# Normalising the attention output first in VectorE's step, in front of the masked maxima

## The chip, the cores and the metric

The kernel runs on one core of a Trainium2 chip. The metric is the device time of one execution in microseconds (us), lower is better. Engines are named as in the profile: PE is TensorE (matmuls), PEld its weight loads, DVE is VectorE, ACT is ScalarE, POOL is GpSimd, SP is SyncE, which here only issues DMAs.

## The reference: a feed-forward pass, windowed attention, a feed-forward pass

Tokens are 8 x 512 rows of width 512. The reference adds three things to them one after the other, each taken from a layer-normalised copy:

```
x = x + 0.5 * ffn(layernorm(x))        # pass A
x = x + attn(layernorm(x))             # attention, pass B
x = x + 0.5 * ffn(layernorm(x))        # pass C

ffn:  gate, up = split(x @ ternary(w_gate_up).T);  h = silu(gate) * up
      return rms_norm(h) @ ternary(w_proj).T                      # hidden width 2048
attn: 32 heads of width 16; a query sees its own and the previous 128 keys
      probs = softmax(where(valid, q @ k.T * scale, min));  return (probs @ v) @ Wo.T
```

## The kernel before

**Blocks and steps.** The rows are cut into 32 blocks of 128 tokens; 4 blocks make a sequence. A prologue of about 150 us turns and quantises the weights. After it the five engines each run their own list of steps, 4 to about 282; eight steps belong to a block, and in one step TensorE does work of several blocks at different stages. The order inside a step is written by hand for each engine (the functions `step_of`), and engines meet only at semaphores. Nothing reorders it.

**TensorE's step.** First half of up for a quarter of a feed-forward pass (`ps_g`), down for the quarter of two steps ago, second half of up (`ps_u`), then scores of a group of 4 heads for the next step, then the product of probabilities and V (`prob_v`) of the group of three steps ago, and in some steps a projection (Q, K, V or output). In the names below `ps_gu` is the pair of banks with `ps_g` and `ps_u`, `ps_yy` holds down's results, `ps_s` scores, and `ps_om` the pair of `ps_o` (product with V) and `ps_m` (projections). Passes A and C have their quarters in alternating steps, so that each step has one; before the first blocks have reached C and after the last has left A, only one of the two passes is there.

**VectorE's step.** The masked maxima of the scores (L876, four pairs: the masked scores to `masked`, the maximum to `row_max`); the low half of Q, K or V in some steps (L854); the low half of the probabilities of the group before (`prob`, L850); in every second step, from step 16 on, the normalisation of the attention output of 8 heads; the gated `hid` (L859: reads `ps_g`, writes `hid`); sometimes the added attention output (L978); the second `hid` (L865: reads `ps_u`); sometimes the low half of the attention output (`oh`), the added feed-forward output (L898) and a layer norm's statistics; last the low half of the hidden values (`hh`).

**The normalisation** is `normalise_o`: it waits for the second product with V of its pair of groups (`p_pv`), sums the two halves of the product (`o_sum`, L886), takes the reciprocal of the row sums (`row_inv`, L887), and multiplies both into `o_norm` (L891). Four of them make a block's attention output. TensorE waits for it (`d_on`) before the next pair of groups overwrites `ps_o`, and after the fourth ScalarE copies `o_norm` to `oh`.

**What waits for what around it.** Scores of the next group overwrite `ps_s`, so TensorE waits for the step's maxima (`d_mx`). ScalarE turns the maxima into `exp_bias`, takes four exponentials in place, later makes `prob` of them. The first half of up in the next step overwrites `ps_g`, so it waits for this step's gated `hid` (`d_gate`). SP transposes each half of the probabilities, the normalised tokens (`xt_A`, `xt_B`, `xt_C`), `hh` and `oh` by DMA, one list for all. GpSimd normalises the tokens (`xhat`, L539) and takes their low half (`xh`, L544).

Of the kernel before, what the change touches and what calls it, by code (L numbers as in the profile page):

```python
# [24 lines left out]
def macaron(nc, x, Wq, Wk, Wv, Wo, w_gate_up, w_proj, out):  # L25
# [47 lines left out]
    NORM = PV + 1  # L73
# [7 lines left out]
    with ExitStack() as ctx:  # L81
# [180 lines left out]
        def need(eng, s, n):  # L262
            if n > 0:
                eng.wait_ge(s, n)

        def block_at(step, offset):

            b, rest = divmod(step - offset, 8)
            return b if rest == 0 and 0 <= b < NB else None

        def group_at(step, offset):

            n = step - offset
            return (n // 8, n % 8) if 0 <= n < 8 * NB else (None, None)
# [49 lines left out]
        def complete(s, step, behind):  # L324

            t, b, c = ffn_at(step - behind)
            return b if t == s and c == NC - 1 else None
# [53 lines left out]
        def head_view(ap):  # L381
            return ap.rearrange("p (h d) -> p h d", d=DK)
# [5 lines left out]
        def prob_part(ap, b):  # L388

            return ap[:, first_half(b):2, :, :]  # L390
# [358 lines left out]
        def _(dve):  # L749
# [132 lines left out]
            def normalise_o(b, ct):  # L882
                dve.wait_ge(p_pv, 8 * b + 2 * ct + 2)
                o = ps_o[:, 0:8 * VW].rearrange("p (h t) -> p h t", h=8)
                parts = o[:, :, 0:2 * DK].rearrange("p h (t d) -> p h d t", t=2)
                dve.tensor_reduce(o_sum[:, :, :], parts, AX.X, ALU.add).then_inc(d_osum, 1)  # L886
                dve.reciprocal(row_inv[:, :].unsqueeze(2), o[:, :, 2 * DK:VW]).then_inc(d_rinv, 1)  # L887
                dve.wait_ge(d_osum, 4 * b + ct + 1)
                dve.wait_ge(d_rinv, 4 * b + ct + 1)
                need(dve, d_ol, b)  # L890
                dve.tensor_tensor(out=head_view(o_norm[:, ct * P:(ct + 1) * P]), in0=o_sum[:, :, :],  # L891
                                  in1=row_inv[:, :].unsqueeze(2).to_broadcast([P, 8, DK]),
                                  op=ALU.mult).then_inc(d_on, 1)
# [50 lines left out]
            attention_scales()  # L944

            def step_of(step):
                b, g = group_at(step, SCORES)
                if b is not None:
                    masked_max(b, g)

                b = block_at(step, Q_AT + 1)
# [3 lines left out]
                b = block_at(step, K_AT + 1)  # L955
# [3 lines left out]
                b = block_at(step, V_AT + 1)  # L959
# [3 lines left out]
                b, g = group_at(step, PROB)  # L963
                if b is not None:
                    need(dve, t_pl[g % 2], 16 * (4 * b + g // 2))
                    take_lo(prob_part(prob[:, g % 2, 1, :, :, :], b), prob_f32(b, g),
                            prob_part(prob[:, g % 2, 0, :, :, :], b), a_ph, 8 * b + g + 1, d_pl)

                b, g = group_at(step, NORM)
                if b is not None and g % 2:  # L970
                    normalise_o(b, g // 2)

                def output_lo(b):
                    take_lo(oh[:, 1, :], o_norm[:, :], oh[:, 0, :], a_oh, b + 1, d_ol)
# [19 lines left out]
                b = block_at(step, WO_AT + 1)  # L994
# [17 lines left out]
                b = block_at(step, SPLIT_O)  # L1012
                if b is not None and b < LAST:
                    output_lo(b)
                b = complete("A", step, 2)
                if b is not None:
                    add_ffn("A", b, d_x1)
                b = complete("C", step, 2)
                if b is not None:
                    add_ffn("C", b, d_x3)  # L1020
                b = block_at(step, LN_B)
                if b is not None and b > 0:
                    norm_stats("B", b, d_x1, b + 1)
                b = block_at(step, LN_C)
                if b is not None and b < LAST:
                    norm_stats("C", b, d_x2, b + 1)
                b = block_at(step, LN_A)
# [9 lines left out]
            for step in range(FIRST_STEP, STEPS):  # L1037
                step_of(step)
# [239 lines left out]
```

## Time and profile before

| | |
|---|---|
| median of 3 runs | 2048.57 us (2048.05 to 2049.78) |
| profiled execution, its time | 2045.48 us |
| its span | 2043.7 us, so 1.8 us lie around it |
| TensorE, VectorE, ScalarE, GpSimd busy | 94%, 78%, 73%, 26% of the span |
| TensorE's mean granted clock | 0.984 of full |

In a row of the timeline the first number is the start in us from the start of the span, the second the duration, then engine, line of the kernel, operation, output and inputs, and the count. What stands in square brackets is the time for which the engine was idle just before, and what ended it; no bracket means that it wasn't. In the list of waits a row is: waiting engine and operation, what it waited for, then the total in us, how many times, the longest. Matmul ends are modelled, and a row's duration can reach 0.1 us over the start of the next on the same engine.

### The profile page before, as it was taken

To read this page: it belongs to the slowest core of one execution; us is meant where nothing else is said; L and a number is where in the kernel's file an instruction comes from. 1 tells how busy PE (TensorE), PEld (TensorE's weight loads), DVE (VectorE), ACT (ScalarE), POOL (GpSimd) and SP (SyncE) were. 2 spreads that over 40 slices of the span, in tenths; PEclk is the share of its full clock that TensorE was granted. 3 is DMA by queue.
4 is the path that set the end of the run, shared out by engine and by line. 5 is a ranking of instruction groups with operands and counts; after the bars stand their busy time and mean duration, and the time that the engine had idled before them with its cause. 6 is when DMAs were issued, how large, how long until landed. Compare 5 with 4: busy or idle time off the path is not lost. (4 is left out here: it accounts for less than half of the span.)

```text
span 2043.7 us, 37471 instructions
## 1 busy us (share of the span) xinstructions
PE 1918.7 (94%) x12447; PEld 897.5 (44%) x12688; DVE 1596.0 (78%) x4079; ACT 1485.7 (73%) x2871; POOL 527.8 (26%) x559
## 2 busy tenths in 40 slices
PE   6588899999999999999999999999999999999887
PEld 4353344444444444444444444444444444444332
DVE  7967788778887888788887888778887788777763
ACT  7837777777777777777776777777776777768762
POOL 2012232222232322322223223222223232221110
PEclk9889999999999999999999999999999999999888
DMA  6336898779887987677886788869886788768762
GB/s 232 125 67 120 150 154 142 126 140 159 149 150 129 153 144 148 134 145 147 154 157 124 137 149 152 148 129 154 157 150 123 139 150 163 141 122 153 135 127 55
DMA packets 1031648, 287.81 MB, mean 141 GB/s; under 512 B 1016096, under 2 KB 1017120, under 8 KB 1030944
## 3 DMA queue, kind: packets, MB, share of 16 engines
q1 hardware_dynamic: 1031456, 285.41, 75.5%
q8 instruction: 101, 1.65, 0.3%
q14 instruction: 91, 0.75, 0.1%
HBM read 25.17 MB, written 8.39 MB: 16 GB/s over the span
## 5 line engine op out<-in xcount | busy, mean ns | idle before, releaser
L731 ACT ACTIVATE masked<-masked,exp_bias,exp_scale 128x256 f32<-128x256 f32 (+1 forms) x1024 | 503.9, 563 | 8.6
L1094 PE MATMUL ps_yy<-wp_t,ht 128*128 128x512 bf16 x1978 | 480.7, 383 | 13.6 <-DMA ht<-hh 11.5
L1048 PE MATMUL ps_gu<-wgu_t,xt_A 128*128 128x512 bf16 x1940 | 473.2, 381 | 10.3 <-DVE hid L859 2.9
L1048 PE MATMUL ps_gu<-wgu_t,xt_C 128*128 128x512 bf16 x1958 | 475.6, 381 | 7.0 <-DVE hid L859 1.1
L605 ACT ACTIVATE hh<-hid 128x512 f16<-128x512 f32 x256 | 160.7, 628 | 271.7 <-DVE hid L865 266.1
L850 DVE TENSOR_TENSOR prob<-masked,prob 128x1024 f16<-128x1024 f32 (+1 forms) x256 | 342.4, 1338 | 9.5 <-ACT prob L743 9.5
L876 DVE CUSTOM_DVE_ANT_0 masked<-ps_s,mask 128x256 f32<-128x256 f32 (+1 forms) x1024 | 337.2, 385 | 0.6 <-PE ps_s L1084 0.6
L865 DVE SCALAR_TENSOR_TENSOR hid<-ps_gu,h_scale_u,hid 128x512 f32<-128x512 f32 x252 | 189.1, 750 | 159.9 <-PE ps_gu L1048 142.5
L1094 PEld LDWEIGHTS ps_yy<-wp_t,ht 128*128 128x128 f16 x2016 | 197.5, 98 | 252.6 <-DMA ht<-hh 13.2
L1048 PEld LDWEIGHTS ps_gu<-wgu_t,xt_A 128*128 128x128 f16 x2048 | 198.2, 98 | 241.8 <-issue 5.3
L1048 PEld LDWEIGHTS ps_gu<-wgu_t,xt_C 128*128 128x128 f16 x2048 | 194.1, 98 | 228.4 <-issue 6.9
L544 POOL TENSOR_TENSOR xh<-xhat,xh 128x512 f16<-128x512 f32 x94 | 132.7, 1412 | 595.1 <-ACT xh L605 595.1
L850 DVE TENSOR_TENSOR hh<-hid,hh 128x512 f16<-128x512 f32 x256 | 176.1, 688 | 129.3 <-ACT hh L605 126.6
L743 ACT ACTIVATE prob<-masked 128x1024 f16<-128x1024 f32 (+1 forms) x256 | 239.3, 935 | 0.5
L609 ACT ACTIVATE hid<-ps_gu 128x512 f32<-128x512 f32 x256 | 150.1, 586 | 86.6 <-PE ps_gu L1048 82.9
L859 DVE SCALAR_TENSOR_TENSOR hid<-hid,ps_gu 128x512 f32<-128x512 f32 x256 | 174.1, 680 | 11.3 <-ACT hid L609 10.9
L1106 PE MATMUL ps_om<-v,pt 128*128 128x33 f16 x3584 | 131.9, 178 | 27.9 <-DVE o_norm L891 26.0
L666 ACT ACTIVATE squares<-hid 128x512 bf16<-128x512 f32 x256 | 157.1, 614 | 0.0
L1106 PEld LDWEIGHTS ps_om<-v,pt 128*128 128x128 f16 x3584 | 107.3, 96 | 77.4 <-issue 71.6
L726 ACT ACTIVATE exp_bias<-row_max,prob_bias,neg_exp_scale 128x4 f32<-128x4 f32 x256 | 97.5, 381 | 11.2 <-DVE row_max L876 8.0
L1084 PE MATMUL ps_s<-kt,qt 48*128 48x256 f16 (+1 forms) x1024 | 93.8, 262 | 10.3 <-DVE row_max L876 10.3
L535 POOL TENSOR_TENSOR rstd_B<-var_eps_B,neg_half 128x1 f32<-128x1 f32 x32 | 28.5, 890 | 282.0 <-DVE var_eps_B L845 282.0
(148 smaller groups left out, 1875.6 us busy)
## 6 DMA issues: line engine op xcount, KB each, us to landing
stream<-in_L_attn_x_dram SPq DMA_DIRECT2D x32, 256.0 KB, 3.4
pt<-prob SPq DMA_TRANSPOSE x512, 3.3
out_dram<-stream SPq DMA_DIRECT2D x32, 256.0 KB, 2.4
prob<-in_L_ffn_w_gate_up_dram SPq DMA_DIRECT2D x4, 1024.0 KB, 5.6
ht<-hh SPq DMA_TRANSPOSE x256, 3.2
stream<-in_L_ffn_w_gate_up_dram SPq DMA_DIRECT2D x3, 1024.0 KB, 5.4
stream<-in_L_ffn_w_proj_dram SPq DMA_DIRECT2D x2, 1024.0 KB, 4.9
prob<-in_L_ffn_w_proj_dram SPq DMA_DIRECT2D x2, 1024.0 KB, 5.4
```

The lines of the kernel that those rows point to most:

```text
L605: act.activation(dst, src, ACT.Copy, scale=scale).then_inc(done, 1)
L609: act.activation(hid[:, n % 2, :], ps_g[:, :], ACT.Tanh, scale=0.5 * 2.0 ** -XS_LOG2).then_inc(a_tanh[s], 1)
L666: act.activation(squares[:, n % 2, :], hid[:, n % 2, :], ACT.Square, accum_out=sq_quarter[s][:, c:c + 1]).then_inc(a_sq[s], 1)
L731: t = act.activation(p, p, ACT.Exp, bias=exp_bias[:, 4 * g + h:4 * g + h + 1], scale=exp_scale[:, 0:1])
L743: act.activation(prob_part(prob[:, g % 2, 0, :, :, :], b), prob_f32(b, g), ACT.Copy).then_inc(a_ph, 1)
L850: dve.tensor_tensor(out=dst, in0=src, in1=hi, op=ALU.subtract).then_inc(done, 1)
L859: dve.scalar_tensor_tensor(out=hid[:, n % 2, :], in0=hid[:, n % 2, :], scalar=1.0, in1=ps_g[:, :], op0=ALU.add, op1=ALU.mult).then_inc(d_g ...
L865: dve.scalar_tensor_tensor(out=dst, in0=ps_u[:, :], scalar=scale, in1=hid[:, n % 2, :], op0=ALU.mult, op1=ALU.mult).then_inc(d_h[s], 1)
L876: m = dve.tensor_tensor_reduce(masked[:, g % 2, 2 * pair + o, first:2 * P], ps_s[:, o * CH + pair * 2 * P + first:o * CH + (pair + 1) * 2 ...
L1048: t = pe.matmul(bank[:, :], xt[s][:, part, k, :], wgu_t[:, k, at:at + CH], start=(k == 0 and part == 0), stop=(k == KD - 1 and part == 1))
L1094: t = pe.matmul(ps_y[s][:, :], ht[:, n % HRING, i, :], wp_t[:, 4 * c + i % 4, :], start=(c == 0 and i == 0), stop=(c == NC - 1 and i == 2 ...
L1106: t = pe.matmul(ps_o[:, at:at + VW], pt[:, g % 2, part, half, 2 * pair + o, :], v[:, at_block - 1 + half, hd, 0:VW], start=(n == 0), stop= ...
```

## The change

In VectorE's step the call of `normalise_o` moves from behind the low half of the probabilities to the head of the step, in front of `masked_max`. Its condition, its waits and its instructions are the same; no other engine's list changes.

```
             def step_of(step):
+                b, g = group_at(step, NORM)
+                if b is not None and g % 2:
+                    normalise_o(b, g // 2)
+
                 b, g = group_at(step, SCORES)
                 if b is not None:
                     masked_max(b, g)
...
                     take_lo(prob_part(prob[:, g % 2, 1, :, :, :], b), prob_f32(b, g),
                             prob_part(prob[:, g % 2, 0, :, :, :], b), a_ph, 8 * b + g + 1, d_pl)
-
-                b, g = group_at(step, NORM)
-                if b is not None and g % 2:
-                    normalise_o(b, g // 2)
```

On VectorE, in a step with the fourth normalisation of a block (`hh` closes the step before, `masked` and `row_max` are the maxima, `ps_om` the product with V); first the whole difference:

```order
 L850 TENSOR_TENSOR hh<-hid,hh 128x512
-L876 ISA masked,row_max<-ps_s,mask 128x256
...
-L850 TENSOR_TENSOR prob<-masked,prob 128x1024
-L886 TENSOR_REDUCE o_sum<-ps_om 128x128
-L887 RECIPROCAL row_inv<-ps_om 128x8
-L891 TENSOR_TENSOR o_norm<-o_sum,row_inv 128x128
+L886 TENSOR_REDUCE o_sum<-ps_om 128x128
+L887 RECIPROCAL row_inv<-ps_om 128x8
+L891 TENSOR_TENSOR o_norm<-o_sum,row_inv 128x128
+L876 ISA masked,row_max<-ps_s,mask 128x256
...
+L850 TENSOR_TENSOR prob<-masked,prob 128x1024
 L859 SCALAR_TENSOR_TENSOR hid<-hid,ps_gu 128x512
```

The three instructions of the normalisation have passed the maxima and the low half of the probabilities; the gated `hid` (L859) stands where it stood, behind all of them.

On VectorE, in a step with the low half of K (`k4`), the same three instructions are also moved past that:

```order
 L850 TENSOR_TENSOR hh<-hid,hh 128x512
+L886 TENSOR_REDUCE o_sum<-ps_om 128x128
+L887 RECIPROCAL row_inv<-ps_om 128x8
+L891 TENSOR_TENSOR o_norm<-o_sum,row_inv 128x128
 L876 ISA masked,row_max<-ps_s,mask 128x256
...
 L854 SCALAR_TENSOR_TENSOR k4<-ps_om,k4 128x32x16
 L850 TENSOR_TENSOR prob<-masked,prob 128x1024
-L886 TENSOR_REDUCE o_sum<-ps_om 128x128
-L887 RECIPROCAL row_inv<-ps_om 128x8
-L891 TENSOR_TENSOR o_norm<-o_sum,row_inv 128x128
 L859 SCALAR_TENSOR_TENSOR hid<-hid,ps_gu 128x512
```

They stand now in front of an instruction that waits for ScalarE's copy of K, where they stood behind it.

## Rows read from the trace of the kernel before

**Rows 1.** The page: span, TensorE's busy time, its granted clock in 40 slices.

```profile
span 2043.7 us, 37471 instructions
...
PE 1918.7 (94%) x12447; PEld 897.5 (44%) x12688; DVE 1596.0 (78%) x4079; ACT 1485.7 (73%) x2871; POOL 527.8 (26%) x559
...
PEclk9889999999999999999999999999999999999888
```

**Rows 2.** Waits of PE, 152 to 240, 240 to 1880, 1880 to 1980 us.

```profile
PE ps_om L1106 <- DVE o_norm L891: 7.7, 5, 1.9
PE ps_s L1084 <- DVE row_max L876: 3.8, 4, 2.4
PE ps_gu L1048 <- DMA xt_A<-xh: 1.3, 2, 0.9
...
PE ps_om L1106 <- DVE o_norm L891: 10.7, 21, 0.7
PE ps_gu L1048 <- DVE hid L859: 1.1, 7, 0.2
...
PE ps_om L1106 <- DVE o_norm L891: 7.6, 6, 2.0
PE ps_s L1084 <- DVE row_max L876: 6.5, 4, 2.2
```

**Rows 3.** Line L891: duration in ns, least, median and most; first and last start.

```profile
L891 DVE TENSOR_TENSOR o_norm<-o_sum,row_inv x128: 291/293/623, 171.9 to 1990.4; 128x128 f32<-128x128 f32 x128
```

**Rows 4.** Timeline, a step with a block's fourth normalisation, all engines.

```profile
1015.97 0.75 DVE L865 SCALAR_TENSOR_TENSOR hid<-ps_gu,h_scale_u,hid 128x512 f32<-128x512 f32 x1 [0.70 <-PE ps_gu L1048]
...
1019.03 0.42 DVE L876 CUSTOM_DVE_ANT_0 masked<-ps_s,mask 128x256 f32<-128x256 f32 x1
...
1019.69 2.08 POOL L539 TENSOR_SCALAR xhat<-stream,mean_var_B,rstd_B 128x512 f32<-128x512 f32 x1 [0.18 <-POOL rstd_B L535]
...
1020.40 0.08 DVE L876 DVE_READ_ACCUMULATOR2_ANT row_max<- 128x1 f32 x1
1020.40 1.22 DVE L850 TENSOR_TENSOR prob<-masked,prob 128x1024 f16<-128x1024 f32 x1
...
1021.54 0.42 DVE L886 TENSOR_REDUCE o_sum<-ps_om 128x128 f32<-128x256 f32 x1
...
1021.77 0.39 PE L1084 MATMUL ps_s<-kt,qt 48*128 48x256 f16 x4
...
1022.16 0.29 DVE L891 TENSOR_TENSOR o_norm<-o_sum,row_inv 128x128 f32<-128x128 f32 x1
1022.37 0.68 DVE L859 SCALAR_TENSOR_TENSOR hid<-hid,ps_gu 128x512 f32<-128x512 f32 x1
...
1022.60 0.55 PE L1106 MATMUL ps_om<-v,pt 128*128 128x33 f16 x16 [0.44 <-DVE o_norm L891]
...
1023.11 1.90 PE L1048 MATMUL ps_gu<-wgu_t,xt_C 128*128 128x512 bf16 x8
```

**Rows 5.** Timeline, the same place in a block with half as many keys.

```profile
379.11 0.68 DVE L859 SCALAR_TENSOR_TENSOR hid<-hid,ps_gu 128x512 f32<-128x512 f32 x1
...
379.85 0.82 PE L1048 MATMUL ps_gu<-wgu_t,xt_C 128*128 128x512 bf16 x3 [0.15 <-DVE hid L859]
```

**Rows 6.** Timeline, the same place where it is tightest: last maximum, scores.

```profile
434.67 0.08 DVE L876 DVE_READ_ACCUMULATOR2_ANT row_max<- 128x1 f32 x1
...
435.75 0.39 PE L1084 MATMUL ps_s<-kt,qt 48*128 48x256 f16 x4
```

**Rows 7.** Timeline near the start: projection Q on PE, low half of K.

```profile
218.93 4.05 PE L1073 MATMUL ps_om<-wq,xt_B 128*128 128x512 f16 x12 [0.66 <-issue]
...
231.01 0.69 DVE L854 SCALAR_TENSOR_TENSOR k<-ps_om,k 128x512 f16<-128x512 f32 x1 [0.85 <-ACT k L605]
```

**Rows 8.** Timeline near the end: first half of up of pass C.

```profile
1974.26 1.68 PE L1048 MATMUL ps_gu<-wgu_t,xt_C 128*128 128x512 bf16 x7 [0.98 <-DMA xt_C<-xh]
```

**Rows 9.** Timeline, GpSimd's low half of xh beside the low half of the probabilities.

```profile
1005.93 1.16 POOL L544 TENSOR_TENSOR xh<-xhat,xh 128x512 f16<-128x512 f32 x1 [5.28 <-ACT xh L605]
1005.97 2.19 DVE L850 TENSOR_TENSOR prob<-masked,prob 128x1024 f16<-128x1024 f32 x1
```

## The prediction

> **What bounds the kernel now.** I first read the page. TensorE is busy for 1918.7 of 2043.7 us, and its granted clock is at the full level in the slices between the edges [rows 1]. So only idle time of TensorE, or a lower clock, can be won or lost, and the next view is the list of TensorE's waits, taken by stretch [rows 2]. It shows three kernels in one. Between 240 and 1880 us TensorE waits for almost nothing: 10.7 us in 21 waits for VectorE's `o_norm`, 1.1 us in 7 waits for VectorE's gated `hid` (L859). Before 240 us it waits 7.7 us in 5 waits for `o_norm` and 3.8 us in 4 for the masked maxima, after 1880 us 7.6 us in 6 and 6.5 us in 4. The `o_norm` waits sum to 26.0 us, which is all that the move can address directly. Last I read one step of the steady stretch in order of time [rows 4]. The reader is to see there which of VectorE's results TensorE takes next after `o_norm`.
>
> **What is moved, and its length.** Three instructions, 128 times: sum, reciprocal and product, from 1021.54 to 1022.16 + 0.29 = 1022.45 us, 0.91 us [rows 4]; the product took 291 to 293 ns in all but a few of its 128 runs, 623 ns at most [rows 3]. No instruction is added, no DMA and no wait. On VectorE they pass the four masked maxima (1.45 us, 1019.03 to 1020.48), in some steps the low part of K or V, and the low part of the probabilities (1.22 us). What they pass becomes 0.91 us later, and `o_norm` becomes up to 2.6 us earlier: before it ended at 1022.45, now it can end at 1019.03 + 0.91 = 1019.94.
>
> **Does the new place wait?** Its only late input is TensorE's product of probabilities and V of the step before (4 matmul groups). VectorE enters a step only behind the low part of `hid`, which hangs on TensorE's second half of up, and that product follows this half by scores and itself alone, about 1 us (1021.77 to 1022.60 with the wait in it, [rows 4]); VectorE still has `hid`, ScalarE's copy and its own low part in front, each of about the length of that product. So it is early, and I cost this at nothing.
>
> **The steady stretch: what is late next.** In the fourth normalisation of a block scores start at 1021.77, the product at 1022.60, and the next step's first half of up at 1023.11 [rows 4]. By the list the product waits 10.7 / 21 = 0.5 us, and that would come free. But up overwrites `ps_g`, and for that TensorE waits until VectorE's gated `hid` has read it. That instruction is from 1022.37 to 1023.05, and up starts at 1023.11, 0.06 us behind it. In the blocks with half as many keys the wait stands in the open: `hid` from 379.11 to 379.79, up at 379.85, again 0.06 us, with a wait of 0.15 us that the trace gives to it [rows 5]; these are the 7 waits of [rows 2]. And gated `hid` doesn't move: from 1019.03 to 1022.37 VectorE runs without a gap, and the order within that run changes, not its length. Even its start is tied, through the `hid` at 1015.97 that waited for TensorE. So TensorE gets `o_norm` 2.5 us earlier and stands 0.5 us later in the same step for the same 1023.05. **Steady stretch: 0**, between 0 and -1.5 us (28 blocks by 0.05 us of rounding). I take 0 here, since the 0.06 us recurs in both kinds of block.
>
> **What the delay could cost there.** Scores need the masked maxima. In the step shown they end at 1020.48 and scores start at 1021.77: 1.29 us of slack against 0.91. The tightest of the steps that are moved is of the kind of [rows 6]: maxima end at 434.67 + 0.08 = 434.75, scores start at 435.75, 1.00 us, so 0.09 us is left; and if it were overdrawn by a few tenths, TensorE would still stand before gated `hid` later. Zero. ScalarE's exponentials start later by part of the 0.91 us in one step of a block, and it then idles for the next `hid` anyway; the transposes of the low part go into SP's queue up to 0.9 us later, with a whole step until TensorE takes them. Zero for both.
>
> **The edges.** Before 240 and after 1880 us one of the two feed-forward passes is missing, TensorE's steps are shorter, and VectorE and ScalarE often set the end. There a wait of TensorE for the maxima stands in front of the one for `o_norm` in the same step or the next; it grows by 0.91 us where the other goes. By [rows 2]: start 7.7 - 4 x 0.91 = 4.1 us, end 7.6 - 4 x 0.91 = 4.0 us, as an upper estimate. Not all is kept. At the start, projection Q at 218.93 waits for VectorE's added attention output [rows 7], which stands behind the same run of work in either order; and the transposed `xt_A` (1.3 us of waits, [rows 2]) comes through SP as before. In favour speaks a second term: where VectorE stood idle for ScalarE's K (0.85 us at 231.01, [rows 7]), the normalisation now lies in that idle time, and all behind it comes earlier. Walking the steps from row to row I keep 2.4 us. At the end the `xt_C` at 1974.26, which waited 0.98 us [rows 8], is queued on SP behind the low part of the probabilities, and that is moved back 0.9 us; I keep 2.3 us of 4.0. **Edges: -4.7 us**, between +2 (every scores wait grows, every `o_norm` wait is replaced) and -9. The clock is below full only at the edges [rows 1]; less idle time there can lift a stretch to the upper level or not. I leave it in the range.
>
> **Sum.** The profiled execution took 2045.48 us, its span 2043.7 and 1.8 us around it. 2045.5 + 0 - 4.7 = 2040.8 us. The median of the runs shown lies 3.1 us higher, at 2048.57; on it the sum is 2043.9 us.
>
> **A rule against the trace.** The product of the normalisation reads two tensors from SBUF. It moves to 0.62 us after the step's start, which is where GpSimd's `xhat` begins (1019.69 against 1019.03, [rows 4]) and runs for 2.08 us. Do the two exclude each other? The low part of the probabilities, which also reads two such tensors, began at 1020.40 in the middle of that `xhat` and took its normal 1.22 us [rows 4]. Beside GpSimd's other operation, the low part of `xh` (two inputs, from 1005.93), the same instruction took 2.19 us [rows 9]. So the trace shows exclusion against the two-input operation, none against `xhat`. The Trainium skill, "SBUF — State Buffer", section "SBUF: two separate sides", says that VectorE and GpSimd share a port pair as an exclusive lock, held for the whole instruction, and names VectorE operations with two SBUF inputs against any GpSimd operation that reads SBUF. By [rows 9] the trace agrees, by [rows 4] it doesn't. By the rule the time would be that of rival B.
>
> **Rivals.**
> A: gated `hid` isn't what holds up; the 0.06 us is a coincidence, and TensorE keeps the half microsecond. For it: the list names `o_norm` in 21 waits and gated `hid` in 7. Against it: the same 0.06 us in both kinds. It gives -10.7 - 4.7 = -15.4, 2033.2 us. Chance 0.09.
> B, the slower one: the product gets behind `xhat` in the fourth normalisation of each block. Its place is the start of VectorE's step; `xhat` would end at 1021.77, the product 0.29 us later instead of at 1019.94, so the maxima, and gated `hid` behind them, are 2.1 us later. The slack of 1.29 us in front of scores is gone from 0.4 us on, and each further delay is TensorE's: 28 x 2.1 = 59 us, less the edges' 4.7: about 2103 us. Against it stands the 1.22 us. A small form of it, where both start together and the product stretches to the 623 ns of [rows 3], gives 28 x 0.33 = 9.2 - 4.7: 2053 us. Chance 0.06 for both.
> C: the edges give back everything, since there the maxima delay ScalarE, and what ScalarE gives bounds the step. For it: scores wait there for 10.3 us already. The time stays within 2 us of 2048.6. Chance 0.10.
>
> **How the numbers follow.** The forecast has 0.75. My measure for no change is 0.2%, 4.1 us, about what a measurement of this kernel can tell. The forecast's own 4.7 us lies just beyond, so I split it 0.44 faster, 0.31 within. With A: faster 0.53. With C: same 0.41. B: slower 0.06. The range takes the forecast's bounds, widened at the low side for the clock and part of A, and at the high side up to C: 2035 to 2049.
>
> **What would show it.** Right: the list of waits between 240 and 1880 us names gated `hid` (L859) some 28 times with about 0.5 us each, and `o_norm` hardly at all; blocks are as long as before; ScalarE's waits for `o_norm` shrink; scores wait longer at the edges, and the sum of TensorE's idle time falls by 4 to 6 us there. Wrong: blocks shorter by half a microsecond (A), a product of 0.6 us or more in the fourth normalisation (B), or the last block ending as far behind as before (C).

## The result: 11 us faster, one forecast wait swapped for another, one term mis-sized, one left out

The changed kernel takes 2037.74 us (median of 5 runs, 2034.24 to 2041.45), against 2048.76 us for the kernel before (5 runs, 2048.05 to 2049.78). The ratio is 0.9949, 95% interval 0.9938 to 0.9960. The forecast was 2043.9, so the direction was right and the gain more than twice as large: 11.0 us for 4.7. A later series timed the changed kernel again, at 2037.38 us and a ratio of 0.9941 (0.9928 to 0.9953).

The profiled execution of the changed kernel took 2037.74 us. From its page, to be read against [rows 1]:

```profile
span 2035.8 us, 37471 instructions
...
PE 1922.4 (94%) x12447; PEld 901.1 (44%) x12688; DVE 1583.7 (78%) x4079; ACT 1493.2 (73%) x2871; POOL 531.4 (26%) x559
...
PEclk9789999999999999999999999999999999999989
```

VectorE is busy for 12.3 us less, with the same instructions: some of them got shorter, which was in no step of the prediction. The grouped lines between 240 and 1880 us name them (busy time, mean ns):

```profile
L850 DVE TENSOR_TENSOR prob<-masked,prob 128x1024 f16<-128x1024 f32 x170 | 243.1, 1430 | 0.0
...
L850 DVE TENSOR_TENSOR prob<-masked,prob 128x512 f16<-128x512 f32 x56 | 51.6, 922 | 0.0
```

The same two rows of the kernel before:

```profile
L850 DVE TENSOR_TENSOR prob<-masked,prob 128x1024 f16<-128x1024 f32 x169 | 247.1, 1462 | 0.0
...
L850 DVE TENSOR_TENSOR prob<-masked,prob 128x512 f16<-128x512 f32 x56 | 58.3, 1041 | 0.0
```

170 x 0.032 + 56 x 0.119 = 12.1 us, all of it on the low part of the probabilities. Only 3.1 us of it are worth time; the experiment on the half-key blocks (those with half as many keys, [rows 5]) tells them apart.

TensorE's waits in the same three stretches (columns as in [rows 2]: total, times, longest), first 152 to 240, then 240 to 1880, then 1880 to 1980 us:

```profile
PE ps_s L1084 <- DVE row_max L876: 5.5, 4, 3.2
...
PE ps_gu L1048 <- DMA xt_A<-xh: 2.0, 2, 1.5
```

```profile
PE ps_gu L1048 <- DVE hid L859: 11.0, 21, 0.7
```

```profile
PE ps_s L1084 <- DVE row_max L876: 10.0, 4, 3.2
PE ps_om L1106 <- DMA pt<-prob: 2.3, 2, 1.9
...
PE ps_gu L1048 <- DMA xt_C<-xh: 1.9, 1, 1.9
```

All waits of TensorE for `o_norm` are gone from the three stretches. ScalarE's waits for it, between 240 and 1880 us, fell from 84.4 to 18.4 us, as the list of what would show it had it. Between 240 and 1880 us, 21 waits of 10.7 us have become 21 waits of 11.0 us for the gated `hid`. At both edges the waits for the maxima grew (3.8 to 5.5, 6.5 to 10.0 us), and transfers that were hidden behind `o_norm` came into the open.

The swap in one step, the fourth normalisation of a block, as in [rows 4] (timeline of the changed kernel; start, duration, engine, line, operation, idle time before and what ended it):

```profile
1018.58 0.29 DVE L891 TENSOR_TENSOR o_norm<-o_sum,row_inv 128x128 f32<-128x128 f32 x1
1018.62 2.20 POOL L539 TENSOR_SCALAR xhat<-stream,mean_var_B,rstd_B 128x512 f32<-128x512 f32 x1 [0.18 <-POOL rstd_B L535]
...
1021.02 0.56 PE L1106 MATMUL ps_om<-v,pt 128*128 128x33 f16 x16
1021.30 0.68 DVE L859 SCALAR_TENSOR_TENSOR hid<-hid,ps_gu 128x512 f32<-128x512 f32 x1
1022.04 1.25 PE L1048 MATMUL ps_gu<-wgu_t,xt_C 128*128 128x512 bf16 x5 [0.45 <-DVE hid L859]
```

The product with V starts without a wait, since `o_norm` ended at 1018.87. Up then stands 0.45 us, and starts 0.06 us behind the end of `hid` (1021.98), the same 0.06 us as before. From the start of the step's `hid` to the start of up it is 0.74 us, as in [rows 4] (1022.37 to 1023.11).

**Where the time went.** I cut every trace at the same pieces of work: first scores, scores of group 16 (counted from 0), scores of group 240, the last product with V. In us, of the profiled executions:

| kernel | prologue | start | steady (group 16 to 240) | end | tail |
|---|---|---|---|---|---|
| before | 152.25 | 88.34 | 1636.70 | 110.07 | 56.3 |
| before, second trace | 153.10 | 91.91 | 1636.76 | 109.87 | 53.4 |
| changed | 153.92 | 86.80 | 1633.89 | 106.46 | 54.7 |
| changed, second trace | 153.91 | 87.49 | 1633.90 | 105.93 | 54.7 |

The steady stretch repeats to 0.1 us, and lost 2.8 us where I forecast 0. Start and end don't repeat as well: two traces of the kernel before differ by 3.6 us at the start. The stretch views of these pieces tell why (length, then busy time with count for PE, PEld, DVE, ACT and POOL, then PEclk, DMA share, GB/s). Before, second trace of before, changed:

```profile
152.25:240.59 88.34, 71.46 (x476) 31.82 (x485) 65.52 (x210) 67.84 (x137) 23.66 (x23) 0.98 0.71 128
1877.29:1987.36 110.07, 90.17 (x653) 40.60 (x665) 80.87 (x222) 79.36 (x148) 16.88 (x21) 0.91 0.74 134
```

```profile
153.10:245.01 91.91, 75.12 (x477) 32.66 (x486) 65.62 (x210) 67.86 (x137) 23.70 (x23) 0.93 0.67 123
1881.77:1991.64 109.87, 90.13 (x654) 40.45 (x665) 80.89 (x222) 79.34 (x148) 16.93 (x21) 0.91 0.74 135
```

```profile
153.92:240.72 86.80, 72.88 (x478) 32.16 (x486) 64.95 (x210) 67.75 (x137) 23.69 (x23) 0.96 0.74 127
1874.61:1981.07 106.46, 89.23 (x653) 40.61 (x665) 81.00 (x222) 79.42 (x147) 16.27 (x21) 0.92 0.79 139
```

The two traces of before have the same idle time of TensorE at the start, 88.34 - 71.46 = 16.9 and 91.91 - 75.12 = 16.8 us. What differs is how long the same matmuls took, at a granted clock of 0.98 or of 0.93. So the edges are better judged by idle time: start 16.9 to 86.80 - 72.88 = 13.9, end 110.07 - 90.17 = 19.9 to 106.46 - 89.23 = 17.2, 3.0 + 2.7 = 5.7 us less. With the second trace of each it is 16.8 to 14.5 and 19.7 to 17.2, 4.8 us. Idle time isn't exact either. Some matmul records are missing from these traces (653 matmuls beside 665 weight loads at the end), and a missing record counts as idle. Two kernels of the experiments have as many matmuls as weight loads at the edges: the half-key kernel, whose edges are those of the kernel before, and the one with the move at the edges alone. Start and end of the first, then of the second:

```profile
153.22:245.19 91.97, 76.04 (x485) 32.64 (x485) 65.58 (x210) 67.85 (x137) 23.65 (x23) 0.93 0.67 123
...
1879.09:1984.57 105.48, 87.80 (x665) 39.83 (x665) 80.88 (x222) 79.35 (x148) 16.89 (x21) 0.94 0.77 140
```

```profile
153.29:238.55 85.26, 71.88 (x486) 31.72 (x486) 64.84 (x210) 67.73 (x137) 23.66 (x23) 0.98 0.72 131
1875.26:1980.62 105.36, 89.54 (x665) 40.35 (x665) 81.04 (x222) 79.66 (x148) 16.07 (x21) 0.92 0.78 140
```

By them idle time falls from 15.9 to 13.4 and from 17.7 to 15.8 us, 4.4 us. So the move takes 4.4 to 5.7 us of idle time out of the edges (forecast 4.7, and 4 to 6 in the list of what would show it).

### The profile page after: what moved, and what is told of

The parts are those of the page before. It is cut to its first block and busy times, and to the rows that moved or that the text cites. A ratio compares the mean times of both kernels' runs of the same rounds, so it can differ in the third digit from the quotient of the medians.

```text
span 2035.8 us, 37471 instructions
## 1 busy us (share of the span) xinstructions
PE 1922.4 (94%) x12447; PEld 901.1 (44%) x12688; DVE 1583.7 (78%) x4079; ACT 1493.2 (73%) x2871; POOL 531.4 (26%) x559
## 5 line engine op out<-in xcount | busy, mean ns | idle before, releaser
L1048 PE MATMUL ps_gu<-wgu_t,xt_C 128*128 128x512 bf16 x1958 | 474.4, 380 | 17.7 <-DVE hid L859 11.0
L1048 PE MATMUL ps_gu<-wgu_t,xt_A 128*128 128x512 bf16 x1940 | 475.7, 383 | 12.2 <-DVE hid L859 3.2
L850 DVE TENSOR_TENSOR prob<-masked,prob 128x1024 f16<-128x1024 f32 (+1 forms) x256 | 330.3, 1290 | 5.4 <-ACT prob L743 5.2
L1094 PEld LDWEIGHTS ps_yy<-wp_t,ht 128*128 128x128 f16 x2016 | 197.8, 99 | 252.8 <-DMA ht<-hh 12.3
L859 DVE SCALAR_TENSOR_TENSOR hid<-hid,ps_gu 128x512 f32<-128x512 f32 x256 | 174.2, 680 | 13.8 <-ACT hid L609 13.6
L1106 PE MATMUL ps_om<-v,pt 128*128 128x33 f16 x3584 | 132.2, 178 | 3.3 <-DMA pt<-prob 3.3
L1106 PEld LDWEIGHTS ps_om<-v,pt 128*128 128x128 f16 x3584 | 106.6, 96 | 51.3 <-issue 44.7
L1084 PE MATMUL ps_s<-kt,qt 48*128 48x256 f16 (+1 forms) x1024 | 93.6, 261 | 15.5 <-DVE row_max L876 15.5
```

The source lines that it names most:

```text
L850: dve.tensor_tensor(out=dst, in0=src, in1=hi, op=ALU.subtract).then_inc(done, 1)
L859: dve.scalar_tensor_tensor(out=hid[:, n % 2, :], in0=hid[:, n % 2, :], scalar=1.0, in1=ps_g[:, :], op0=ALU.add, op1=ALU.mult).then_inc(d_g ...
L1048: t = pe.matmul(bank[:, :], xt[s][:, part, k, :], wgu_t[:, k, at:at + CH], start=(k == 0 and part == 0), stop=(k == KD - 1 and part == 1))
L1094: t = pe.matmul(ps_y[s][:, :], ht[:, n % HRING, i, :], wp_t[:, 4 * c + i % 4, :], start=(c == 0 and i == 0), stop=(c == NC - 1 and i == 2 ...
L1106: t = pe.matmul(ps_o[:, at:at + VW], pt[:, g % 2, part, half, 2 * pair + o, :], v[:, at_block - 1 + half, hd, 0:VW], start=(n == 0), stop= ...
```

## The experiments

Each kernel is compared with the kernel before as timed in the same series; that took 2047.24, 2048.18 and 2048.24 us in the three series. The ratios are to that, with their 95% intervals; stretches are compared with the table above. `gated` is the call that issues the gated `hid`; in a step with a block's fourth normalisation, `step % 8` is 6. An inserted line moves the later ones of a kernel by up to 4, so L1110 is L1106 of before.

### Half-key blocks alone

Only 7 steps differ from the kernel before, all in the steady stretch: those in which a block's fourth normalisation meets scores of a block with half as many keys.

```
+                b, g = group_at(step, NORM)
+                if b is not None and g % 2 and ((28 <= step < 254) and b % 4 == 3 and g == 7):
+                    normalise_o(b, g // 2)
                 b, g = group_at(step, SCORES)
...
                 b, g = group_at(step, NORM)
-                if b is not None and g % 2:
+                if b is not None and g % 2 and not ((28 <= step < 254) and b % 4 == 3 and g == 7):
                     normalise_o(b, g // 2)
```

> The normalisation goes to the head only in seven steps, the fourth normalisation where the scores have half as many keys (steps 46, 78, ... 238). Theory 1 (there the low part of the probabilities started 0.2 us behind GpSimd's xhat and was held 0.45 us; behind the normalisation it starts 1.0 us after it and isn't): the instruction takes 0.69 instead of 1.13 us in these seven steps, up of the next step starts 0.4 us earlier, 7 x 0.40 = 2.8 us less, about 2045.9 on a median of 2048.7. Theory 2 (the gain of those blocks comes from other steps of theirs, which now have the normalisation first too): the time stays within 0.5 us, whatever that instruction takes.

Measured: 2040.98 us, 0.9968 (0.9956 to 0.9981). The steady stretch took 1633.90 us, 2.80 us less than before, which is the whole difference of the changed kernel there. A block with half as many keys takes 56.60 us for 57.00, and every other kind takes what it took: 7 x 0.40 = 2.8. What got shorter is in the timelines of that step. The kernel before:

```profile
377.06 2.08 POOL L539 TENSOR_SCALAR xhat<-stream,mean_var_B,rstd_B 128x512 f32<-128x512 f32 x1 [0.18 <-POOL rstd_B L535]
...
377.24 1.13 DVE L850 TENSOR_TENSOR prob<-masked,prob 128x512 f16<-128x512 f32 x1
```

The changed kernel:

```profile
377.15 0.29 DVE L891 TENSOR_TENSOR o_norm<-o_sum,row_inv 128x128 f32<-128x128 f32 x1
377.19 2.20 POOL L539 TENSOR_SCALAR xhat<-stream,mean_var_B,rstd_B 128x512 f32<-128x512 f32 x1 [0.18 <-POOL rstd_B L535]
...
378.20 0.69 DVE L850 TENSOR_TENSOR prob<-masked,prob 128x512 f16<-128x512 f32 x1
...
379.59 1.02 PE L1048 MATMUL ps_gu<-wgu_t,xt_C 128*128 128x512 bf16 x4
```

With half the keys the maxima are short, and the low part of the probabilities began 0.18 us behind GpSimd's `xhat`: it took 1.13 us for its usual 0.69. With the normalisation ahead of the maxima it begins 0.83 us later, 1.01 us behind `xhat`, and takes 0.69; in the half-key kernel's own trace it is the same, 1.01 us behind and 0.69 us long. So 0.44 us of VectorE's time goes, the gated `hid` ends earlier by it, and up starts (379.59) without a wait.

VectorE's busy time in the steady stretch fell by 3.1 us in this kernel (1308.68 to 1305.57) and by 12.2 us in the changed one (to 1296.46), and the stretch is as long in both. So the other 9 us bring nothing. They lie beside `xh`, GpSimd's other operation. It lengthens the low part of the probabilities as long as that begins early ([rows 9]); behind the normalisation it begins later and is shorter, 1.88 us for 2.19 in 13 steps, and no block gets shorter by it. The time of the whole kernel fell by more, 6.3 us; that is taken up below.

### The same kernel again, with a second trace

> The kernel with the seven steps again, as a second trace and a second set of times. Theory 1 (its further 3.5 us were chance of the clock in that set): 2.8 us below before, within 1.5 us. Theory 2 (they are systematic): again 6 to 7 us below before. The steady stretch is 1633.9 us in both.

Measured: 2041.77 us, 0.9962 (0.9949 to 0.9976), steady stretch 1633.98. The 6.5 us repeat the 6.3, so it isn't chance. In the traces the end is shorter, though this kernel's code there is that of before: 105.55 us (105.48 in its first trace) for 110.07 and 109.87. Against the second trace of before, 1.1 us each come back in the prologue and the tail, so the profiled executions are 4.6 us apart. The end of this kernel in the stretch view, to be read against the two of the kernel before above; then the projection V on PE, first in the kernel before, then in this one:

```profile
1880.38:1985.93 105.55, 86.87 (x653) 39.85 (x665) 80.90 (x222) 79.35 (x148) 16.89 (x21) 0.94 0.77 142
```

```profile
1928.18 0.56 PE L1084 MATMUL ps_s<-kt,qt 48*128 48x256 f16 x4 [2.00 <-DVE row_max L876]
...
1929.15 3.99 PE L1073 MATMUL ps_om<-wv,xt_B 128*128 128x512 f16 x12
```

```profile
1931.06 0.39 PE L1088 MATMUL ps_s<-kt,qt 48*128 48x256 f16 x4 [2.02 <-DVE row_max L876]
...
1931.80 2.75 PE L1077 MATMUL ps_om<-wv,xt_B 128*128 128x512 f16 x12
```

The same 12 matmuls, after the same wait of 2 us, took 3.99 us at a mean granted clock of 0.68, part of them at the lower level (1.2 GHz), and 2.75 us at the full level (2.4 GHz). Over the end stretch TensorE's busy time fell from 90.17 to 86.87, 3.3 us, at a mean clock of 0.94 for 0.91, and idle time by 1.2 us. In the 26 us ahead (before, then this kernel) TensorE had been busy for 21.48 us in the one and 21.35 us in the other, at full clock in both:

```profile
1902.00:1928.00 26.00, 21.48 (x161) 9.94 (x160) 19.93 (x54) 18.69 (x34) 4.81 (x7) 1.00 0.84 148
```

```profile
1905.00:1931.00 26.00, 21.35 (x161) 9.92 (x160) 19.98 (x56) 18.77 (x34) 4.93 (x7) 1.00 0.84 149
```

So 2.8 us are the program's, and the end is some 4.5 us shorter, of which the larger part went with the clock. That all three traces with this end and the shorter steady stretch have it (the third is the next kernel's), and both traces of before don't, is measured; why the clock fell in one and not in the other isn't shown by anything here. That something ahead got shorter isn't needed for it, as the kernel with the gated `hid` ahead shows below.

### The move in the steady stretch alone

```
+                if b is not None and g % 2 and (28 <= step < 254):
+                    normalise_o(b, g // 2)
...
-                if b is not None and g % 2:
+                if b is not None and g % 2 and not (28 <= step < 254):
                     normalise_o(b, g // 2)
```

> The counterpart of the run with the edges alone: the normalisation at the head only in the steady steps 28 to 253. Theory 1 (in the steady stretch the move pays only in the seven blocks with half as many keys, by 0.4 us each): steady stretch 1633.9 us, TensorE's waits at the edges as before, so 2.8 us by the program; the median within 2 us of that, 2044 to 2046. Theory 2 (any change of the steady stretch by a few us also moves the edges against the granted clock, and that gave the run with the seven steps its further 3.5 us): the same steady stretch, but a median near 2041 and fewer us at the lower clock than in the two traces of before.

Measured: 2039.95 us, 0.9953 (0.9940 to 0.9965). Steady 1633.91, start 91.96 and end 105.28: start and end are those of the half-key kernel, and so is the time: its second theory, near 2041 us, held, and not the 2044 to 2046 us of the first. The moved normalisations of the stretch other than those seven bring nothing; they only rename 21 waits.

### The move at the edges alone

```
+                if b is not None and g % 2 and (not (28 <= step < 254)):
+                    normalise_o(b, g // 2)
...
-                if b is not None and g % 2:
+                if b is not None and g % 2 and not (not (28 <= step < 254)):
                     normalise_o(b, g // 2)
```

> The normalisation goes to the head of VectorE's step only in steps below 28 and from 254 on (the edges); in the 226 steps between it stays where it was. Theory 1 (the move pays at the edges, and in the steady stretch only 2.8 us, in seven blocks): the two traces put 1.5 us at the start, 3.6 us up to the last product and 1.6 us in the tail, so 6.7 us faster than before by the profile, between 5 and 9, TensorE waits for o_norm in the steady stretch as before (about 10.7 us in 21). Theory 2 (most of the 11 us between the medians comes from the steady stretch): at most 3 us faster.

Measured: 2039.81 us, 0.9963 (0.9950 to 0.9975). Steady 1636.71, as before to 0.01 us; start 85.26, end 105.36. The edges gain 7.4 us by the medians (6.7 expected, and 4.7 in the prediction). With the steady part alone (8.3 us) that makes 15.7, more than the 11.0 of both. A part at the end seems to be gained by either and can't be gained twice: the two traces of before have 110 us there, and each of these kernels 105 to 106. That reading is argued, not shown.

### The gated hid ahead, without the change

This is the test of the rival that the gated `hid` isn't what holds TensorE next. The normalisation stays where it was; in the step of the fourth one the gated `hid` goes in front of the low part of the probabilities.

```
+                s, bf, c, n = gate_at(step)
+                if s and (28 <= step < 254 and step % 8 == 6):
+                    gated(s, bf, c, n)
...
-                if s:
+                if s and not (28 <= step < 254 and step % 8 == 6):
                     gated(s, bf, c, n)
```

> The normalisation stays where it was; in the steady steps with a block's fourth normalisation the gated hid goes in front of the low part of the probabilities, so it is 1.2 + 0.9 us earlier and the normalisation 0.6 us later. Theory 1 (TensorE stands first for o_norm, then for gated hid, and either alone holds it): the wait for o_norm becomes 0.5 + 0.6 us, up of the next step starts some 0.5 us later than before, 28 x 0.5 = 14 us slower, about 2062; none of TensorE's waits in the steady stretch is for gated hid. Theory 2 (only gated hid holds TensorE): 28 x 0.5 = 14 us faster, about 2034.

Measured: 2054.81 us, 1.0039 (1.0026 to 1.0051), steady 1645.62, so +8.9 us. TensorE's waits between 240 and 1880 us, and the step:

```profile
PE ps_om L1110 <- DVE o_norm L891: 24.6, 28, 1.3
```

```profile
1031.27 0.55 PE L1110 MATMUL ps_om<-v,pt 128*128 128x33 f16 x16 [1.04 <-DVE o_norm L891]
1031.67 1.67 PE L1052 MATMUL ps_gu<-wgu_t,xt_C 128*128 128x512 bf16 x7
```

The sign is right and the size was missed, +8.9 for +14. The product's wait grew by 0.60 us (0.44 in [rows 4]), but up now follows the product after 0.40 us, where it followed after 0.51 while it still waited for `hid`: 0.49 a block, 10.3 us for 21. The half-key blocks gain 0.16 each, 1.1 in all. Freeing `hid` alone wins nothing in a block with all keys, as long as the normalisation is late.

This kernel also settles whether the end needs something shorter ahead of it. The code of its edges is that of before, and its steady stretch is 8.9 us longer. Its end:

```profile
1889.98:1997.71 107.73, 89.93 (x665) 40.35 (x665) 80.70 (x222) 79.14 (x148) 16.89 (x21) 0.92 0.75 137
```

107.73 us for 110.07 and 109.87, at a mean clock of 0.92. So, over six traces, the same code at the end took 110 us behind a steady stretch of 1637 us, 105 to 106 behind one of 1634, and 108 behind one of 1646: not in the order of the lengths.

### Both: the change, and the gated hid ahead

The same edit on the changed kernel, with the normalisation at the head of the step in all steps.

```
+                if b is not None and g % 2:
+                    normalise_o(b, g // 2)
...
+                if s and (28 <= step < 254 and step % 8 == 6):
+                    gated(s, bf, c, n)
...
-                if s:
+                if s and not (28 <= step < 254 and step % 8 == 6):
                     gated(s, bf, c, n)
```

> The normalisation at the head in all steps, as in the change, and in addition, in the steady steps with a block's fourth normalisation, the gated hid in front of the low part of the probabilities. Theory 1 (after the change gated hid is what TensorE waits for in these steps, 11.0 us in 21 waits): these waits go, 11 to 13 us less than the changed kernel, about 2026; blocks of 58.5 instead of 59.07 us. Theory 2 (another result is as late as gated hid, such as the second hid or the scores' maxima): less than 4 us below the changed kernel, 2034 to 2041, with a new wait in the list.

Measured: 2023.75 us, 0.9884 (0.9870 to 0.9897), steady 1619.50. With the two kernels above this is a table of two by two. Steady stretch against before: `hid` ahead alone +8.9, normalisation ahead alone -2.8, both -17.2 us. In the blocks with all keys neither alone frees TensorE, both together do: between 240 and 1880 us TensorE has two waits left, of 3.0 and 0.2 us, and both lie behind group 240, in the end. Rival A fell by this, and the step on what is late next holds: it was the gated `hid`, worth 14.4 us once moved. Expected were 11 to 13 us, by waits of 11.0; where the other 3.4 us come from isn't shown.

### The kernel before, unchanged, once more

> The kernel before, unchanged, as a second trace and as a control. Theory 1 (the edges of the profiled executions differ by where the granted clock is low, whatever the kernel): same as before within 0.1% in the medians; in the trace the steady stretch, from the 17th to the 241st group of scores, is again 1636.7 us, while the 110.1 us from there to the last product with V, and the 88.3 us in front, may move by several us. Theory 2 (the kernel before is always slow at its end): the end is again near 110 us and what follows near 56 us.

Measured: 2047.26 us, 0.9996 (0.9988 to 1.0005). Its trace is the second row of the table above. Its steady stretch is that of the first trace to 0.1 us; start and tail differ from it by 3.6 and 3.0 us, so a single trace tells no smaller difference there. The end doesn't differ, 109.87 for 110.07, as the second theory had it.

### The normalisation between the maxima and the low part

```
                     masked_max(b, g)
+                b, g = group_at(step, NORM)
+                if b is not None and g % 2:
+                    normalise_o(b, g // 2)
...
-                b, g = group_at(step, NORM)
-                if b is not None and g % 2:
-                    normalise_o(b, g // 2)
```

> The normalisation between the masked maxima and the low part of the probabilities, in all steps: o_norm is 1.2 us earlier than before and not 2.6, and the maxima are where they were. Theory 1 (scores at the edges wait longer for the maxima in the changed kernel, and that gives part of the gain back): steady stretch 1633.9 us as in the changed kernel (no hold behind xhat either), TensorE's waits for the maxima at the edges 10.3 us as before instead of 15.5, time 2 to 5 us below the changed kernel. Theory 2 (what is given back there would be lost anyway to other waits): within 1.5 us of the changed kernel.

Measured: 2037.86 us, 0.9950 (0.9937 to 0.9962), the changed kernel's time. The maxima are no longer put back, yet nothing is won by it: steady 1634.22 with `hid` named 21 times for 11.3 us, start 89.75, end 106.20. At the edges the waits for the maxima are 3.6 us less than in the changed kernel (11.9 for 15.5), and 3.2 us of waits for `o_norm` are back. The delay of the maxima, which was costed at nothing in the steady stretch, is worth nothing measurable in the whole.

### That, and the gated hid ahead

```
                     masked_max(b, g)
+                b, g = group_at(step, NORM)
+                if b is not None and g % 2:
+                    normalise_o(b, g // 2)
...
+                s, bf, c, n = gate_at(step)
+                if s and (step % 8 == 6):
+                    gated(s, bf, c, n)
...
-                if s:
+                if s and not (step % 8 == 6):
                     gated(s, bf, c, n)
```

> The normalisation between the maxima and the low part of the probabilities, and, in the steps with a block's fourth normalisation, the gated hid behind it, in front of the low part. Theory 1 (two separate waits of TensorE, each taken away): steady stretch 1619.5 us as in the run with the normalisation at the head and gated hid early, no wait of TensorE for o_norm or gated hid there, 14 to 16 us below the run with the normalisation in the middle alone. Theory 2 (the order maxima, normalisation, gated hid makes gated hid no earlier than needed): steady stretch between 1620 and 1634 us.

Measured: 2022.97 us, 0.9885 (0.9870 to 0.9901), steady 1619.48. Of all orders timed this one and the other with both moves are the fastest, 23 to 25 us below the kernel before and 14 to 15 below the changed one (14 to 16 expected), and the two can't be told apart. Its step with a fourth normalisation:

```profile
1008.49 0.29 DVE L891 TENSOR_TENSOR o_norm<-o_sum,row_inv 128x128 f32<-128x128 f32 x1
1008.70 0.68 DVE L859 SCALAR_TENSOR_TENSOR hid<-hid,ps_gu 128x512 f32<-128x512 f32 x1
1009.23 0.39 PE L1088 MATMUL ps_s<-kt,qt 48*128 48x256 f16 x4
1009.30 1.22 DVE L850 TENSOR_TENSOR prob<-masked,prob 128x1024 f16<-128x1024 f32 x1
1009.55 0.56 PE L1110 MATMUL ps_om<-v,pt 128*128 128x33 f16 x16
1009.96 0.81 PE L1052 MATMUL ps_gu<-wgu_t,xt_C 128*128 128x512 bf16 x3
```

`hid` ends at 1009.38, up starts at 1009.96 for other reasons: 0.58 us of slack where 0.45 us of wait stood. The low part of the probabilities (1.22 us), which only its transposes wait for, has gone behind both results that TensorE takes next.

### The gated hid ahead in every step

```
-                if s and (step % 8 == 6):
+                if s and (True):
                     gated(s, bf, c, n)
...
-                if s and not (step % 8 == 6):
+                if False:
                     gated(s, bf, c, n)
```

> As the run before it, but the gated hid stands in front of the low part of the probabilities in every step. Theory 1 (gated hid holds TensorE only in the step with the fourth normalisation): steady stretch within 0.5 us of the run before it, time within 2 us. Theory 2 (the low part of the probabilities, 0.7 us later in every step, becomes what is late, through SP's queue): waits of TensorE for transposed probabilities, some us slower.

Measured: 2029.38 us, 0.9906 (0.9892 to 0.9919). The steady stretch is the same to 0.1 us (1619.55), so the move pays in one step of eight only. It loses 6.4 us against the kernel above by the medians. The two traces are further apart, by 10.4 us, since that of the kernel above is its fastest run; 5.4 of these lie at the end, 111.41 for 106.01 us. There TensorE's busy time is 92.65 for 88.54 us at a clock of 0.88 for 0.92, and its idle time 18.8 for 17.5; the transposed probabilities are waited for, 3.7 us in 3 waits (2.3 us in 2 above). So the second theory is right for the end, though most of the loss there is busy time at the lower clock.

### The changed kernel, unchanged, once more

> The changed kernel again, as a second trace. Theory 1 (the program's own gain is 2.8 us in the steady stretch and 4 to 6 at the edges, the rest is the clock at the edges): steady stretch 1633.9 us, waits at the edges as in the first trace, the length of both edges together between 190 and 200 us depending on the lower clock in them. Theory 2 (the edges' gain is fixed): the edges within 0.5 us of the first trace, 86.8 and 106.5 us.

Measured: 2037.38 us, 0.9941 (0.9928 to 0.9953). Its trace is the last row of the first table: steady 1633.90, the idle time of the start 87.49 - 72.97 = 14.5, of the end 105.93 - 88.69 = 17.2 us. The edges together are 193.4 us, for 193.3 in the first trace.

## Why the prediction was right, and what it missed

- **The new place doesn't wait, the normalisation stays 0.91 us: right.** The three instructions run from 1017.95 to 1018.87, 0.92 us, with no wait in front.
- **What is late next: right, and it is the main step.** The waits moved one to one, 10.7 us in 21 to 11.0 us in 21. "Some 28 times" was 21: the half-key blocks have no wait at all any more. The two by two table makes it a cause and not a coincidence of 0.06 us.
- **Steady stretch 0: wrong by 2.8 us, and the step that failed is the reading of GpSimd's `xhat`.** "The order within that run changes, not its length" was read in a block with all keys; in the half-key blocks the length changed too, by 0.44 us. I looked at a block with all keys, where the low part of the probabilities begins 0.71 us behind `xhat` and took 1.22, and wrote that the trace shows no exclusion against it. In the half-key blocks the same operation stood 0.18 us behind it and took 1.13 for 0.69. I had looked at that step too ([rows 5]), but only at its end. The bound for this term, -1.5, was too narrow for the same reason.
- **The product of the normalisation beside `xhat` (rival B): didn't come, and by less than I knew.** In those steps it starts 0.04 us ahead of `xhat`, keeps its 0.29 us, and `xhat` takes 2.20 us for 2.08. Nothing here says what would have come 0.04 us later, except that the low part of the probabilities was held there.
- **The delay of the maxima: right, 0.** No wait for scores appeared between 240 and 1880 us, and the kernel that doesn't delay them takes the same time.
- **The edges: right, in kind and in size as far as the traces can tell.** 4.4 to 5.7 us of TensorE's idle time went, for 4.7. Waits for the maxima grew by 1.7 and 3.5 us, less than the 15.3 us of `o_norm` waits that went, and `xt_A`, `xt_C` and the probabilities' transposes took back part, as the step on [rows 7, 8] had it. Rival C fell.
- **The clock: left out of the sum, and it shouldn't have been.** The program accounts for 2.8 us and 4.4 to 5.7 us, together 7.2 to 8.5 of the 11.0. The half-key kernel had 3.3 us less of busy time in an unchanged end. So a term of 2 to 4 us for the clock belongs in the sum, by size; its sign can't be forecast from anything here, and what decides it stays open. The traces don't hold the whole of the 11.0 either: the profiled executions differ by 7.5 to 9.3 us (2045.48 and 2046.99 for 2037.74 and 2037.96), since the first of before ran 3.3 us below its median.

The range held because it was widened at the low side for the clock and for part of A, not because its centre was right: the centre was 6.2 us too high. That the 11.0 us lie inside it is in part luck.

## What to carry to other kernels

When a wait is removed, look for the next semaphore of the waiting engine in the same step and how far in front of its start that one comes; if it is the other engine's next instruction, move both or expect nothing. Here one move alone left 21 of 28 blocks as long as they were, the other made them 0.49 us longer, and both together took 17.2 us off. Order an in-order engine's step by who is waiting: the two results that TensorE takes next first, the one that only a transfer waits for behind them. And read every kind of block: here the whole gain in the steady stretch lay in one kind of four.

## What the runs showed of the hardware

**GpSimd holds VectorE, but only at the start of the instruction.** In all steps of the traces of before and of the changed kernel, a low part of the probabilities (two tensors from SBUF) that began 0.2 us behind the start of `xhat` took 1.13 to 1.15 us (23 times, for 0.69 alone), one that began 0.6 us behind took 1.26 or 1.27 (3 times, for 1.22 alone), two that began level with it took 0.71, and of those that began 0.7 us behind or later all of the long form took 1.22 and all of the short one 0.68 or 0.69. So the hold ends about 0.63 us behind the start of an instruction of 2.08 us: 0.18 + 1.13 - 0.69 = 0.62, and 0.6 + 1.26 - 1.22 = 0.64. Beside `xh`, which reads two tensors itself, the hold lasted longer: the low part in [rows 9] took 0.97 us more than alone, which ends the hold 1.01 us behind the start of the 1.16 us of `xh`. The Trainium skill, "SBUF — State Buffer", section "SBUF: two separate sides", has the two engines' shared port as the one point on the engine side where they contend. The trace agrees on the point of contention. That section of the Trainium skill has the lock held for the whole instruction; `xh` agrees with that nearly, with 1.01 us of 1.16, and `xhat` doesn't, with 0.63 us of 2.08. Here the measurement decides, with one reserve: the profile's spans on GpSimd are rough, so that the hold is over by then is shown, and what GpSimd did in the rest of the 2.08 us isn't.

**The clock at the edges isn't a constant of a kernel.** Two traces of one kernel had 0.98 and 0.93 over the same work at the start, 71.46 and 75.12 us of busy time. The Trainium skill, "TensorE: Matmul & The Clock Gate", section "Part 1: The HAM clock gate (the "warmup" mystery)", says that the monitor runs free of the kernel's start, so that the same kernel varies. That agrees with the start. It doesn't by itself give a difference that came back at the end: 0.91 in both traces of before, 0.94 in all three traces of the kernels with a steady stretch 2.8 us shorter, and 0.92 where it was 8.9 us longer.
